# An adaptive-LayerNorm attention block with a gated low-rank adapter: one small matrix of gates for four rank groups, and context products spread between other work

## The chip, the cores and the metric

The kernel runs on one core of a Trainium2 chip. The metric is the device time of one execution in microseconds (us). The core's engines run side by side, each in its own program order, and wait for each other on semaphores: TensorE (PE in the profile, its weight loads PEld), VectorE (DVE), ScalarE (ACT), GpSimd (POOL), and SyncE (SP), which here issues the DMA transfers.

## What is computed

Input x has 1024 tokens of 512 columns, everything in float32. `c` gives six modulation vectors of 512 columns (shift and scale for two LayerNorms, and the gates ga and gb).

```
h = layernorm(x) * (1 + ca) + sa
q, k, v = h @ wq.T + bq, h @ wk.T + bk, h @ wv.T + bv     # 32 heads of 16 columns
# attention is over the 32 heads of one token, not over tokens
scores = einsum('bshd,bstd->bsht', q, k) / sqrt(16)
context = einsum('bsht,bstd->bshd', softmax(scores), v)
x = x + ga * context
h = layernorm(x) * (1 + cb) + sb
A_eff = einsum('bn,nri->bri', gate, lora_A)   # 8 groups b of 128 tokens, 16 adapters n, rank r = 32
B_eff = einsum('bn,nor->bor', gate, lora_B)
delta = einsum('bor,btr->bto', B_eff, einsum('bri,bti->btr', A_eff, h))
      + (h @ lora_A_shared.T) @ lora_B_shared.T
x = x + gb * (h @ kernel + bias + delta)
```

## The kernel before

**Tiling.** Tokens are handled in two halves of 512, and in eight groups of 128 in the second part. Each engine's order is written out by hand, in one function per engine. PSUM has eight banks of 128 x 512 float32; the list that `bank_plan` makes gives every use its bank in turn. TensorE's `take` waits until the use eight places earlier in that list has been emptied; the letter in the list says who empties it ("a" ACT, "v" DVE), and `emptied` counts in that order.

**Precision.** The projections and the last product split both operands into a high and a low part and take three passes of 512 columns. All other products are plain float32. Such a product appears in the trace as two passes, each with its own weight load; a transposition is one pass.

**First part.** LayerNorm, transposition, projections. For attention, k and v are copied by DMA into block-diagonal matrices `diag` (one per half), so that one product serves several tokens. `scores(k)`, softmax in four chunks per half (DVE maximum, POOL subtraction, ACT exponential, DVE sum, POOL multiplication, DVE `turn`), then `context(k)` (L1112): 64 products per half with 64 stationary columns (two slots of 32 heads) and 128 moving columns. One product writes partitions 0 to 63, the next 64 to 127. Half of what each computes pairs a slot with the other slot's values. ACT (`ctx_low_part`, L645) and DVE (`ctx_high_part`, L909) pick the right half with a mask, one pass each for every one of 16 banks, and POOL (`gate_ctx`, L488) multiplies by ga (`ga_col`).

**Order of TensorE around the change.** v of the second half (four banks), context(0), transposed lora_B (`b_t`), the two shared adapter matrices (`as_t`, `bs_t`), the transposed context of half 0 (`ctx_t`), `b_eff`, context(1), then for the second part `h2_t(0)`, `a_eff` chunks between halves of ctx_t(1), `h2_t(1)`, and the loop over eight token groups: `ax` (the adapter's first product), the output product with kern_hi and kern_lo, and two passes with `b_rows` (the adapter's second product).

**The adapter.** `gmix` holds gates: 128 rows (four adapters by 32 ranks) by 128 columns for each of four adapter groups and two halves of the token groups. `b_eff` and `a_eff` sum four such products per bank. The rows of `b_rows` are: own high part, own low part, shared high part, shared low part, each 32 partitions. SP fills them by DMA from `b_raw_hi`, `b_raw_lo` (L424, L426) and, for the shared rows, from `tail_hi` and `tail_lo` (L416, L418).

**Between the parts.** DVE adds the transposed context to x (`add_x`, L943), takes the statistics, normalises four token groups (L779), then `b_raw_lo`, then context(1)'s `ctx_high_part`. ACT does `h2_t` (modulation), `h2_high_part`, and `take_a`, which copies `a_eff` into `a_cat`. `split_h2` (L949) on DVE makes the low part of h.

## Time and profile before

| | |
|---|---|
| time of three runs | median 190.35 us (190.28 to 192.47) |
| the profiled execution | 191.63 us, of which the span from first to last instruction is 189.8 us |
| busy share of the span | PE 95%, PEld 81%, DVE 63%, ACT 55%, POOL 46% |
| instructions | 3335 in all; 1326 passes on PE |
| mean granted TensorE clock | 0.99 of full speed |

A row of a timeline gives the start and the length in us, the engine, the line of the kernel, the operation, the tile written and the tiles read, and how many instructions were merged into the row. In brackets stands how long the engine sat idle before and what ended that. Passes on PE are pipelined and overlap, so the time from one row's start to the next is the better measure of what a row cost.

### The profile page before, as it was taken

Reading aid. Unit: us, or ns where it says so; the run is one execution under the profiler, and the core shown is the slowest. Engines: PE = TensorE matmul, PEld = TensorE weight load, DVE = VectorE, ACT = ScalarE, POOL = GpSimd, SP = SyncE. Lnnn points to the kernel's source line nnn. Section 1 sums busy time; section 2 is a strip of 40 time slices with the busy share of each in tenths; the row PEclk is TensorE's granted clock in tenths of the full one; section 3 lists DMA queues with packets and bytes.
Section 4 is the critical chain, followed back from the end, with each engine's and each line's share of the span. In section 5 each row is a group of like instructions: output and inputs, shape, how many; then the busy total and the mean of one; then the engine's idle time right before and its main releaser. Section 6 shows DMA issues by size and latency. Waiting matters only on the chain.

```text
span 189.8 us, 3335 instructions
## 1 busy us (share of the span) xinstructions
PE 180.8 (95%) x1326; PEld 154.6 (81%) x1326; DVE 120.4 (63%) x193; ACT 104.5 (55%) x177; POOL 87.4 (46%) x59
## 2 busy tenths in 40 slices
PE   6997999799999999999999999999999899999993
PEld 6997778688778898888799879964989688888892
DVE  4674994792193277972026977579948587955543
ACT  8623914995124688354366486795674445444410
POOL 1000797099600297984007994945199042420000
PEclk9999699999999999999999999999999999999999
DMA  4999998968197059599859937969690001111112
GB/s 125 372 299 271 301 388 262 409 157 106 45 129 102 3 96 122 78 164 134 89 96 130 297 146 232 185 132 264 176 122 4 0 2 55 55 60 55 61 68 94
DMA packets 24848, 27.95 MB, mean 147 GB/s; under 512 B 12000, under 2 KB 16480, under 8 KB 24192
## 3 DMA queue, kind: packets, MB, share of 16 engines
q1 hardware_dynamic: 24832, 27.74, 63.1%
q8 instruction: 10, 0.16, 0.4%
q14 instruction: 6, 0.05, 0.1%
HBM read 17.24 MB, written 2.10 MB: 102 GB/s over the span
## 4 chain that ended last, share of the span: by engine, by line
PE 76%; DVE 10%; DMA 6%; POOL 3%; SPq 2%; issue 2%; ACT 2%; DVEq 0%
PE ps L1024 15%; PE ps L1026 15%; PE ps L1025 15%; PE ps L1108 8%; PE ps L1016 7%; DMA wm_attn<-in_L_wmod_dram 6%; PE ps L1205 4%; PE ps L1122 4%; PE ps L1161 3%; POOL ctx_c L491 3%; DVE xres L943 2%; DVE xn L779 1%; DVE wk_lo L792 1%; DVE wk_hi L789 1%; DVE stats L768 1%
## 5 line engine op out<-in xcount | busy, mean ns | idle before, releaser
L452 POOL MEMSET diag<- 128x2048 f32 x8 | 14.4, 1823 | 20.8 <-PE ps L1016 20.7
L477 POOL TENSOR_TENSOR steps<-steps,rmax 128x1024 f32<-128x1024 f32 x8 | 15.3, 1925 | 12.0 <-DVE rmax L889 12.0
L447 POOL TENSOR_TENSOR hT_lo<-h_full,hT_hi 128x512 fp32r<-128x512 f32 x8 | 12.1, 1528 | 18.5 <-ACT hT_hi L554 18.5
L698 ACT ACTIVATE h_full<-ps,modc 128x128 f32<-128x128 f32 x32 | 12.1, 456 | 13.3 <-PE ps L1016 13.3
L519 POOL TENSOR_TENSOR xres<-xres,bias_bc 128x512 f32<-128x512 f32 x8 | 12.3, 1563 | 13.0 <-DVE xn L779 13.0
L484 POOL TENSOR_TENSOR steps<-steps,rinv 128x1024 f32<-128x1024 f32 x8 | 15.3, 1918 | 3.8 <-DVE rinv L899 3.8
L889 DVE TENSOR_REDUCE rmax<-steps 128x32 f32<-128x1024 f32 x8 | 9.6, 1199 | 11.8 <-ACT steps L525 11.8
L562 ACT ACTIVATE k<-ps,b_col 128x512 f32<-128x512 f32 x8 | 9.3, 1184 | 12.6 <-PE ps L1026 10.2
L1108 PEld LDWEIGHTS ps<-diag,q 128*64 128x64 f32 x256 | 14.6, 192 | 1.2 <-issue 1.2
L1108 PE MATMUL ps<-diag,q 128*64 128x128 f32 x256 | 14.9, 277 | 0.6 <-issue 0.6
L1122 PEld LDWEIGHTS ps<-diag,steps 128*64 128x64 f32 x256 | 13.9, 137 | 1.1 <-issue 1.1
L1122 PE MATMUL ps<-diag,steps 128*64 128x128 f32 x256 | 14.4, 273 | 0.0
L628 ACT ACTIVATE steps<-steps 128x1024 f32<-128x1024 f32 x8 | 8.5, 1066 | 10.0 <-POOL steps L477 10.0
L1024 PE MATMUL ps<-kern_lo,h_hi 128*128 128x512 f32 (+1 forms) x36 | 14.0, 388 | 0.0
L1024 PE MATMUL ps<-hT_lo,wk_hi 128*128 128x512 f32 x32 | 13.6, 426 | 0.4 <-DVE wk_lo L792 0.4
L491 POOL TENSOR_TENSOR ctx_c<-ctx_c,ga_col 128x512 f32<-128x512 f32 x8 | 10.0, 1282 | 8.4 <-DVE ctx_c L913 8.4
L1026 PE MATMUL ps<-kern_hi,h_hi 128*128 128x512 f32 (+1 forms) x36 | 13.3, 370 | 0.0
L1025 PE MATMUL ps<-kern_hi,h_lo 128*128 128x512 f32 (+1 forms) x36 | 13.2, 366 | 0.0
L895 DVE TENSOR_REDUCE rsum<-steps 128x32 f32<-128x1024 f32 x8 | 9.7, 1216 | 5.3 <-ACT steps L628 5.3
L568 ACT ACTIVATE v<-ps,b_col 128x512 f32<-128x512 f32 x8 | 9.3, 1187 | 6.7 <-PE ps L1026 6.6
L1026 PE MATMUL ps<-hT_hi,wk_hi 128*128 128x512 f32 x32 | 12.7, 398 | 0.0
L1025 PE MATMUL ps<-hT_hi,wk_lo 128*128 128x512 f32 x32 | 12.7, 397 | 0.0
(140 smaller groups left out, 460.0 us busy)
## 6 DMA issues: line engine op xcount, KB each, us to landing
wm_next<-in_L_wmod_dram SPq DMA_DIRECT2D x3, 1024.0 KB, 8.9
x<-_attn_hidden_states_dram SPq DMA_DIRECT2D x8, 256.0 KB, 8.3
wm_attn<-in_L_wmod_dram SPq DMA_DIRECT2D x4, 512.0 KB, 7.7
diag<-k SPq DMA_DIRECT2D x16, 128.0 KB, 4.7
q<-q SPq DMA_DIRECT2D x16, 128.0 KB, 4.9
diag<-v SPq DMA_DIRECT2D x8, 256.0 KB, 7.3
xres<-_attn_hidden_states_dram SPq DMA_DIRECT2D x2, 1024.0 KB, 10.0
out_dram<-xres SPq DMA_DIRECT2D x7, 256.0 KB, 2.0
```

The source lines that it names most:

```text
L447: nc.gpsimd.tensor_tensor(hT_lo[k][:, c], h_full[:, c], hT_hi[k][:, c].bitcast(F32), ALU.subtract).then_inc(h_split, 1)
L452: nc.gpsimd.memset(diag_s[k][:, s, :], 0.0).then_inc(diag_zero, 1)
L477: nc.gpsimd.tensor_tensor(rows, rows, rmax[:, c % 2 * RCH:(c % 2 + 1) * RCH].unsqueeze(2).to_broadcast([P, RCH, H]), ALU.subtract).then_in ...
L484: nc.gpsimd.tensor_tensor(rows, rows, rinv[:, c % 2 * RCH:(c % 2 + 1) * RCH].unsqueeze(2).to_broadcast([P, RCH, H]), ALU.mult).then_inc(no ...
L491: nc.gpsimd.tensor_tensor(part, part, ga_col[:].unsqueeze(1).unsqueeze(1).to_broadcast([P, QUAD, n * GB, D]), ALU.mult).then_inc(ctx_gated, 1)
L519: nc.gpsimd.tensor_tensor(x_j, x_j, bias_bc[:], ALU.add).then_inc(biased, 1)
L1016: ins = nc.tensor.transpose(dst[0:m, n * k:(n + 1) * k], src, ident[0:k, 0:k])
L1024: nc.tensor.matmul(dst, a_hi, b_lo, start=start, stop=False)
L1025: nc.tensor.matmul(dst, a_lo, b_hi, start=False, stop=False)
L1026: return nc.tensor.matmul(dst, a_hi, b_hi, start=False, stop=stop)
L1108: ins = nc.tensor.matmul(dst[r, n * P:(n + 1) * P].rearrange("p (e c) -> p e c", c=IC), q2_g[:, g], diag_k[k][:, g], start=True, stop=True)
L1122: ins = nc.tensor.matmul(to[r, n], pT_g[k][:, g, r], diag_v[k][:, g, 2 * y:2 * y + 2], start=True, stop=True)
```

## The change

One `gmix` of 128 rows (16 adapters by 8 ranks) and 64 columns (8 ranks by 8 token groups) serves four groups of ranks. lora_A and lora_B are read in with their ranks regrouped so. `b_eff` becomes four products of 64 stationary and 512 moving columns, two side by side in one bank; `a_eff` becomes, per bank, four products of 128 stationary and 64 moving columns without summing. `context(c)` is now called for one softmax chunk at a time: 32 products with 32 stationary and 64 moving columns, whose outputs go to four different groups of 32 partitions, and which compute only what is needed. Eight banks hold what sixteen held. The masks and the passes on ACT and POOL go away; DVE's `gate_ctx` reads the bank and multiplies by ga. The eight calls of context stand between v, b_t, a_eff and h2_t. The shared B rows are made in partitions 64 to 127 (by a product with doubled `bs_nat`, in place of transpositions) and copied by POOL to all token groups, in place of two DMA transfers. ACT normalises token groups 2 and 3 in place of DVE; DVE's `b_raw_lo` moves ahead of the statistics; ACT's `kern_hi` moves ahead of `b_t`, and `take_a(0)`, `take_a(1)` ahead of `h2_t(0)`.

```diff
@@ bank_plan
-    uses += [("v", i, "a") for i in half(1, IC)]
-    uses += [("ctx", s, "v") for s in half(0, NSH)]
...
+    uses += [("v", IC, "a"), ("v", IC + 1, "a"), ("ctx", 0, "v"), ("v", IC + 2, "a"), ("ctx", 1, "v")]
...
@@ SP
-            sp.dma_start(la_nat, lora_a.rearrange("(c n) r i -> (n r) c i", n=NG)).then_inc(la_in, 16)
+            sp.dma_start(la_nat, lora_a.rearrange("n (e g) i -> (n e) g i", g=NRG)).then_inc(la_in, 16)
             v_to_diagonal(1)
-            sp.wait_ge(psum_written, written("ctx", NSH - 1))
-            sp.wait_ge(tail_hi_made, 1)
-            sp.dma_start(b_rows[2 * rank:3 * rank].bitcast(F32), tail_rows(tail_hi)).then_inc(b_tail_in, 16)
-            sp.wait_ge(*emptied("bs_t", 0))
-            sp.dma_start(b_rows[3 * rank:4 * rank].bitcast(F32), tail_rows(tail_lo)).then_inc(b_tail_in, 16)
             sp.wait_ge(v_diag_in[1], 16 * QUAD)
             sp.dma_start(xr[1], x_rows[:, NBH:NB, :]).then_inc(x_again[1], 16)
+            sp.wait_ge(psum_written, written("ctx", NCH - 1))
             for q in range(2):
-                tiles = slice(NG * q, NG * (q + 1))
+                own = slice(q * rank // 2, (q + 1) * rank // 2)
...
-                sp.dma_start(b_rows[0:rank, tiles, :].bitcast(F32), b_raw_hi[:, q, :].bitcast(F32)).then_inc(b_eff_in[q], 16)
+                sp.dma_start(b_rows[own].bitcast(F32), b_raw_hi[:, q, :].bitcast(F32)).then_inc(b_eff_in[q], 16)
...
@@ POOL
-            for s in range(0, NSH, 2):
-                gate_ctx(s, 2)
             pool.wait_ge(kern_hi_made, 1)
             nc.gpsimd.tensor_tensor(kern_lo, kern_nat, kern_hi.bitcast(F32), ALU.subtract).then_inc(kern_split, 1)
-            for s in range(NSH, 2 * NSH, 2):
-                gate_ctx(s, 2)
+            pool.wait_ge(kern_split, 1)
+            pool.wait_ge(psum_written, written("ctx", NCH - 1))
+            pool.wait_ge(tail_hi_made, 1)
+            pool.wait_ge(*emptied("bs_t", 0))
+            nc.gpsimd.tensor_copy(b_rows[2 * rank:], tail[2 * rank:, :].bitcast(F32).unsqueeze(1)
+                                  .to_broadcast([2 * rank, NB, hid])).then_inc(tails_made, 1)
...
@@ ACT
+            deviations(2, 0, 2)
+            deviations(3, 2, 4)
+            act.wait_ge(shift_ready, 2)
+            for n, j in enumerate((2, 3)):
+                nc.scalar.activation(xn2[:, j, :], xr[0][:, j, :], ACT.Identity, bias=shift[:, n:n + 1],
+                                     scale=rstd[:, j:j + 1]).then_inc(xn_by_act, 1)
...
+            take_a(0)
+            take_a(1)
             h2_t(0)
             h2_high_part(0)
-            take_a(0)
-            take_a(1)
-            h2_t(1)
             take_a(2)
             take_a(3)
+            h2_t(1)
@@ DVE
+            def gate_ctx(c):
+                dve.wait_ge(psum_written, written("ctx", c))
+                steps_c = slice(c % NCH * 2 * GB, (c % NCH + 1) * 2 * GB)
+                nc.vector.tensor_tensor(ctx_q[:, :, steps_c, :],
+                                        bank("ctx", c).rearrange("p (q g d) -> p q g d", q=QUAD, d=D),
+                                        ga_col[:].unsqueeze(1).unsqueeze(1).to_broadcast([P, QUAD, 2 * GB, D]),
+                                        ALU.mult).then_inc(dve_emptied, 1)
...
@@ PE
+            def context(c):
+                k, n0 = c // NCH, c % NCH * 2 * GB
+                if c % NCH == 0:
+                    pe.wait_ge(v_diag_in[k], 16 * QUAD)
+                pe.wait_ge(turned, c + 1)
+                to = take("ctx", c).rearrange("p (q g e c) -> p g q e c", q=QUAD, g=2 * GB, c=IC)
+                for n in range(2 * GB):
+                    for s in range(SLOT):
+                        r = slice(s * H, (s + 1) * H)
+                        ins = nc.tensor.matmul(to[r, n], pT_g[k][:, n0 + n, r], diag_v[k][:, n0 + n, s],
+                                               start=True, stop=True)
+                ins.then_inc(psum_written, 1)
...
-                for c in range(IC):
-                    ins = nc.tensor.matmul(dst, gmix[:, c, i * P:(i + 1) * P], b_t[:, c, :],
-                                           start=(c == 0), stop=(c == IC - 1))
+                for n in range(2):
+                    ins = nc.tensor.matmul(dst[n * P // 2:(n + 1) * P // 2, :], gmix[:], b_t[:, 2 * i + n, :],
+                                           start=True, stop=True)
...
-                    for c in range(IC):
-                        ins = nc.tensor.matmul(dst[:, 0:NB * rank], la_nat[:, c, i * P:(i + 1) * P], gmix[:, c, :],
-                                               start=(c == 0), stop=(c == IC - 1))
+                    for g in range(NRG):
+                        n = slice(g * GROUP * NB, (g + 1) * GROUP * NB)
+                        ins = nc.tensor.matmul(dst[:, n], la_nat[:, g, i * P:(i + 1) * P], gmix[:],
+                                               start=True, stop=True)
...
                 if j == 0:
-                    pe.wait_ge(b_tail_in, 16 * 2)
-                if j % NG == 0:
-                    pe.wait_ge(b_eff_in[j // NG], 16 * 2)
+                    pe.wait_ge(tails_made, 1)
+                    for q in range(2):
+                        pe.wait_ge(b_eff_in[q], 16 * 2)
```

How TensorE's order moves, from b_eff to the loop over the token groups. A row is a line, an operation, the tile written and the tiles read, the size written, and a count of equal instructions. First before, from b_eff (L1152) on; L1122 is context(1), L1161 is a_eff, and L1016 is a transposition (of `xn` for h2_t, of `ctx_c` for ctx_t(1)):

```order
L1152 MATMUL ps<-b_t,gmix 128x512 x8
L1122 MATMUL ps<-diag_57,steps_101 64x8x16 x64
L1016 MATMUL ps<-ident,xn_58 128x128 x4
L1161 MATMUL ps<-gmix,la_nat 128x256 x4
L1016 MATMUL ps<-ident,ctx_c 128x128 x8
L1161 MATMUL ps<-gmix,la_nat 128x256 x4
L1016 MATMUL ps<-ident,ctx_c 128x128 x8
L1016 MATMUL ps<-ident,xn_58 128x128 x4
L1161 MATMUL ps<-gmix,la_nat 128x256 x8
L1205 MATMUL ps<-h_full,a_cat_98 128x128 x2
```

And of the change, the same stretch from b_eff (now L1148); L1107 is one chunk of context, L1157 a_eff, L1002 a transposition:

```order
L1148 MATMUL ps<-b_t,gmix 64x512 x4
L1107 MATMUL ps<-diag_57,steps_100 32x4x16 x32
L1157 MATMUL ps<-gmix,la_nat 128x64 x4
L1107 MATMUL ps<-diag_57,steps_100 32x4x16 x32
L1157 MATMUL ps<-gmix,la_nat 128x64 x4
L1107 MATMUL ps<-diag_57,steps_100 32x4x16 x32
L1002 MATMUL ps<-ident,xn_58 128x128 x4
L1107 MATMUL ps<-diag_57,steps_100 32x4x16 x32
L1157 MATMUL ps<-gmix,la_nat 128x64 x8
L1002 MATMUL ps<-ident,ctx_c 128x128 x16
L1002 MATMUL ps<-ident,xn_58 128x128 x4
L1204 MATMUL ps<-h_full,a_cat_97 128x128 x2
```

h2_t(0) now stands ahead of the last chunk of context, and all of ctx_t(1) behind the last a_eff.

How DVE's order moves between the statistics of half 0 and add_x of half 1. Before, from the second normalisation (L779); L964 is b_raw_lo, L913 `ctx_high_part`, L943 add_x, L949 split_h2:

```order
L779 SCALAR_TENSOR_TENSOR xn_58<-xres_83,mv,rstd 128x512 x2
L964 TENSOR_TENSOR b_raw_lo<-ps,b_raw_hi 128x512 x2
L913 SCALAR_TENSOR_TENSOR ctx_c<-ps,half_mask,ctx_c 128x4x64 x8
L943 TENSOR_TENSOR xres_84<-ps,xres_84 128x4x128 x2
L949 TENSOR_TENSOR h_lo<-h_full,h_hi 128x512
L943 TENSOR_TENSOR xres_84<-ps,xres_84 128x4x128 x2
```

And of the change, from the one normalisation that is left (L764); L949 and L950 make rstd and shift for ACT, L895 is `gate_ctx`, L932 split_h2, L926 add_x:

```order
L764 SCALAR_TENSOR_TENSOR xn_58<-xres_82,mv,rstd 128x512 x2
L949 RECIPROCAL rstd<-std 128x2
L950 SCALAR_TENSOR_TENSOR shift<-mv,rstd 128x2
L895 TENSOR_TENSOR ctx_c<-ps,ga_col 128x4x128 x3
L932 TENSOR_TENSOR h_lo<-h_full,h_hi 128x512
L895 TENSOR_TENSOR ctx_c<-ps,ga_col 128x4x128
L926 TENSOR_TENSOR xres_83<-ps,xres_83 128x4x128 x4
```

split_h2(0) now stands ahead of the last gate_ctx, and the four steps of add_x behind both.

## Rows read from the trace of the kernel before

**Rows 1.** Page: busy time and share of TensorE; group of POOL memsets with mean ns.

```profile
PE 180.8 (95%) x1326; PEld 154.6 (81%) x1326; DVE 120.4 (63%) x193; ACT 104.5 (55%) x177; POOL 87.4 (46%) x59
...
L452 POOL MEMSET diag<- 128x2048 f32 x8 | 14.4, 1823 | 20.8 <-PE ps L1016 20.7
```

**Rows 2.** Chain that ended last, 113 to 152 us: start, length, what.

```profile
137.14 4.99 POOL ctx_c L491 x4
...
146.41 3.47 PE ps L1161 x16
```

**Rows 3.** Timeline of PE, 14 to 152 us: start, length, stationary*shape, moving size, passes.

```profile
16.07 1.95 PE L1059 MATMUL ps<-ones,wm_attn 128*128 128x1 f32 x16 [1.09 <-DVE wm_attn L819]
...
102.71 0.50 PE L1024 MATMUL ps<-hT_lo,wv_hi 128*128 128x512 f32 x1
...
113.80 7.21 PE L1122 MATMUL ps<-diag,steps 128*64 128x128 f32 x128
120.94 1.97 PE L1016 MATMUL ps<-ident,lb_nat 128*128 128x128 f32 x16
...
123.20 0.61 PE L1016 MATMUL ps<-ident,bs_nat 128*32 128x128 f32 x4
123.65 2.06 PE L1016 MATMUL ps<-ident,ctx_c 128*128 128x128 f32 x16
125.55 7.03 PE L1152 MATMUL ps<-b_t,gmix 128*128 128x512 f32 x16
...
150.61 1.16 PE L1205 MATMUL ps<-h_full,a_cat 128*128 128x128 f32 x8 [0.75 <-ACT a_cat L718]
151.53 0.48 PE L1024 MATMUL ps<-kern_lo,h_hi 128*128 128x512 f32 x1
```

**Rows 4.** Chain that ended last, 48 to 53 us: passes of one column.

```profile
49.09 1.68 PE ps L1088 x16
```

**Rows 5.** Timeline of DVE, 116 to 156 us.

```profile
116.51 1.25 DVE L907 STREAM_TRANSPOSE steps<-steps 128x1024 f32<-128x1024 f32 x1 [0.93 <-POOL steps L484]
...
125.08 3.92 DVE L943 TENSOR_TENSOR xres<-ps,xres 128x512 f32<-128x512 f32 x4
...
132.14 1.42 DVE L779 SCALAR_TENSOR_TENSOR xn<-xres,mv,rstd 128x512 f32<-128x512 f32 x2
...
135.00 1.28 DVE L964 TENSOR_TENSOR b_raw_lo<-ps,b_raw_hi 128x512 fp32r<-128x512 f32 x2
...
144.93 1.45 DVE L949 TENSOR_TENSOR h_lo<-h_full,h_hi 128x512 fp32r<-128x512 f32 x1
...
155.09 0.69 DVE L994 TENSOR_TENSOR gated<-ps,gb_bc 128x512 f32<-128x512 f32 x1
```

**Rows 6.** Timeline of ACT, 112 to 149 us.

```profile
112.74 2.40 ACT L568 ACTIVATE v<-ps,b_col 128x512 f32<-128x512 f32 x2
...
124.35 1.89 ACT L671 ACTIVATE kern_hi<-kern_nat 128x2048 fp32r<-128x2048 f32 x1
...
127.66 2.04 ACT L676 ACTIVATE a_cat<-ps 128x512 f32<-128x512 f32 x4
...
146.45 1.51 ACT L698 ACTIVATE h_full<-ps,modc 128x128 f32<-128x128 f32 x4 [0.68 <-PE ps L1016]
148.17 0.66 ACT L718 ACTIVATE a_cat<-ps 128x256 f32<-128x256 f32 x2 [0.22 <-PE ps L1161]
```

**Rows 7.** ACT groups by form: count, busy us, mean ns.

```profile
L580 ACT ACTIVATE x<-x,shift,rstd 128x512 f32<-128x512 f32 x3 | 2.2, 805 | 0.4 <-DVE shift L806 0.4
```

**Rows 8.** Timeline of POOL, 120 to 132 us.

```profile
126.32 4.56 POOL L513 TENSOR_TENSOR kern_lo<-kern_nat,kern_hi 128x2048 fp32r<-128x2048 f32 x1 [2.73 <-ACT kern_hi L671]
```

**Rows 9.** DMA issues, 117.14 to 117.6 us: KB, us to landing.

```profile
diag<-v SPq DMA_DIRECT2D x1, 256.0 KB, 8.7
```

**Rows 10.** DMA issues, 137.5 to 137.7 us.

```profile
b_rows<-b_raw_lo SPq DMA_DIRECT2D x1, 256.0 KB, 6.0
```

**Rows 11.** Stages: us, busy of five engines, clock, DMA share, GB/s.

```profile
18.90:22.30 3.40, 3.40 (x14) 2.88 (x13) 3.30 (x6) 3.40 (x6) 2.11 (x2) 0.52 1.06 258
```

More of the change, by code:

```diff
@@ L169, in adaln_block @@
         ones = sb("ones", P)
[L170 to L171 removed]
+        lora_mask = sb("lora_mask", lora_n)
+        group_mask = sb("group_mask", GROUP)
         root = sb("root", 1)
@@ L660, in _ @@
             project_v(IC + 3)
-            for s in range(NSH):
-                ctx_low_part(s)
+            act.wait_ge(kern_in, 16)
+            act.wait_ge(psum_written, written("v", 2 * IC - 1))
+            nc.scalar.activation(kern_hi, kern_nat, ACT.Copy).then_inc(kern_hi_made, 1)
             for i in range(IC):
@@ L666, in _ @@
             act.wait_ge(psum_written, written("bs_t", 0))
-            nc.scalar.activation(tail_hi[0:rank, :], bank("bs_t", 0)[0:rank, :], ACT.Copy).then_inc(tail_hi_made, 1)
-            act.wait_ge(kern_in, 16)
-            act.wait_ge(psum_written, written("v", 2 * IC - 1))
-            nc.scalar.activation(kern_hi, kern_nat, ACT.Copy).then_inc(kern_hi_made, 1)
+            nc.scalar.activation(tail[2 * rank:, :], bank("bs_t", 0)[2 * rank:, :], ACT.Copy).then_inc(tail_hi_made, 1)
             nc.scalar.activation(root[:], eps[:], ACT.Sqrt)
@@ L930, in _ @@
                     turn(c - 2)
-            for s in range(NSH):
-                ctx_high_part(s)
+            for c in range(NCH):
+                gate_ctx(c)
             dve.wait_ge(tail_hi_made, 1)
-            nc.vector.tensor_tensor(tail_lo[0:rank, :], bank("bs_t", 0)[0:rank, :], tail_hi[0:rank, :].bitcast(F32),
+            nc.vector.tensor_tensor(tail[3 * rank:, :], bank("bs_t", 0)[3 * rank:, :], tail[3 * rank:, :].bitcast(F32),
                                     ALU.subtract).then_inc(dve_emptied, 1)
@@ L956, in _ @@
             add_x(0, range(2, NCT))
+            for i in range(2):
+                dve.wait_ge(b_hi_made, i + 1)
+                nc.vector.tensor_tensor(b_raw_lo[:, i, :], bank("b_eff", i), b_raw_hi[:, i, :].bitcast(F32),
+                                        ALU.subtract).then_inc(dve_emptied, 1)
             dve.wait_ge(*emptied("ctx_t", NCT - 1))
@@ L960, in _ @@
             normalise(2, 0, 2, to_xn2, xr)
-            normalise(3, 2, 4, to_xn2, xr)
-            for i in range(2):
-                dve.wait_ge(b_hi_made, i + 1)
-                nc.vector.tensor_tensor(b_raw_lo[:, i, :], bank("b_eff", i), b_raw_hi[:, i, :].bitcast(F32),
-                                        ALU.subtract).then_inc(dve_emptied, 1)
-            for s in range(NSH, NSH + 4):
-                ctx_high_part(s)
-            for s in range(NSH + 4, 2 * NSH):
-                ctx_high_part(s)
-            add_x(1, range(2))
+            dve.wait_ge(std_ready, 4)
+            link(nc.vector.reciprocal(rstd[:, 2:4], std[:, 2:4]))
+            nc.vector.scalar_tensor_tensor(out=shift[:, 0:2], in0=mv_v[:, 2:4, 0], scalar=-1.0, in1=rstd[:, 2:4],
+                                           op0=ALU.mult, op1=ALU.mult).then_inc(shift_ready, 1)
+            dve.wait_ge(psum_written, written("ctx_t", NCT - 1))
+            for c in range(NCH, 2 * NCH - 1):
+                gate_ctx(c)
             split_h2(0)
-            add_x(1, range(2, NCT))
+            gate_ctx(2 * NCH - 1)
+            add_x(1, range(NCT))
             dve.wait_ge(*emptied("ctx_t", 2 * NCT - 1))
@@ L1184, in out_part @@
                                  start=False, stop=True).then_inc(psum_written, 1)
-            h2_t(0)
+            context(NCH)
             pe.wait_ge(la_in, 16)
             a_eff([0])
-            ctx_t(1, range(2))
+            context(NCH + 1)
             a_eff([1])
-            ctx_t(1, range(2, NCT))
+            context(NCH + 2)
+            h2_t(0)
+            context(NCH + 3)
+            a_eff([2, 3])
+            ctx_t(1, range(NCT))
             h2_t(1)
-            a_eff(range(2, IC))
             for j in range(NB):
```

140 lines of the change are left out of this document (53 added, 87 removed).

## The prediction

> **What bounds the kernel now.** I read the busy shares first: PE is busy for 180.8 us, 95% of the span [rows 1]. So the question is which PE work goes away, and whether PE finds its inputs in time once it has less to do. The chain of waits that ended last, read for the stretch of the change, runs through PE, but between the two contexts it leaves PE: DVE's add_x and normalisation, and POOL's gating (four passes, 4.99 us from 137.14) lie on it, then PE's a_eff [rows 2]. Both paths are about equally long there. The PE timeline gives what each piece costs [rows 3]. The four v projections of half 1 last from 102.71 to 113.80, 2.77 us each; context(0) 113.80 to 120.94, 7.14; b_eff 125.55 plus 7.03; the first output product (out(0)) starts at 151.53, after 0.75 us of waiting for ACT. From there the loop is PE's own to the end, so I look for the new start of out(0).
>
> **What PE loses and gains.**
> - b_eff: 16 passes of 512 columns in 7.03 us [rows 3], 0.43 each. Now 8 passes, of which two always write different halves of the partitions. Do such passes run side by side? Context shows it: 128 passes of 128 columns in 7.14 us are 0.056 each, while four passes with only 32 stationary columns, all to the same partitions, take 123.20 to 123.65, 0.11 each [rows 3]. A narrow pass is thus no faster alone, and two on different halves take the time of one. So 4 x 0.43 = 1.75 us, 5.3 less (3.5 if they took turns).
> - a_eff: 32 passes of 256 columns; the last 16 take 3.47 us [rows 2], 0.87 a bank. Now 64 columns, with full weights of 128 columns. What such a pass costs at least is seen where it moves one column: 16 passes in 1.68 us, 0.105 [rows 4]. With 0.11 a bank costs 0.9 instead of 1.75 us: 3.4 less in all.
> - bs_t: four transpositions become eight passes of 128 columns to the same partitions, at 0.11: 0.45 more.
> - Context: 64 products of 128 columns per half become 128 products of 64 columns, 256 passes. No row shows four groups of 32 partitions or a pass every 14 ns. Lower bound: all four groups side by side as the two are now; a pass of 64 columns then takes half as long, and four run at once: a quarter of 0.056, 14 ns each, 3.6 us a half. Upper bound: no pass starts faster than today's mean, 0.056, and a half takes 14.3 us. In between lies "no gain", 7.1 us. I take the lower bound, because the side-by-side running that it needs is what rows 3 show for two groups, plus 0.25 us for each of the eight calls, which now stand among other forms (estimate: 16 transpositions take 123.65 to 125.55, 0.119 each, against 0.112 for four narrow ones, so a start costs about 0.1). A call of context is then 0.9 + 0.25 = 1.15 us.
>
> **The path to out(0).** PE alone would gain 5.3 + 3.4 - 0.45 + 14.3 - 9.2 = 13.3 us. It cannot have all of this, since the others come in.
> - v4, v5, context 0, v6, context 1, v7: 102.71 + 11.1 + 2.3 = 116.1, 2.3 later than before. ACT empties v7 by 117.2, 2.1 later than 115.14 [rows 6]; kern_hi (1.89) follows.
> - Context 2 to 117.2; three b_t transpositions (sixteen took 1.9, [rows 3]) to 118.7. The fourth needs the bank of context 0, which DVE empties only behind its last `turn`, 116.51 + 1.25 = 117.76 [rows 5]; gate_ctx, a pass of 512 columns from PSUM, I price as the like pass at 155.09, 0.69 [rows 5]: 118.45. No wait. The two masks and POOL's gating go from the chain here. Context 3, as_t (0.36) and bs_t (0.9 + 0.1): 121.7, which in the trace was 123.65. tail_hi and tail_lo, 0.65 each, and DVE starts add_x at about 122.9, 2.2 earlier than 125.08 [rows 5].
> - From add_x to the end of the first two normalisations DVE took 125.08 to 133.56 [rows 5], 8.5 us; b_raw_lo (1.28) is now inside: 132.7. ACT hands it b_raw_hi in time: tail_hi to 122.3, the table load and a_cat 3.46 (from 126.24, the end of kern_hi, to 129.70, [rows 6]), two copies 1.1: 126.9, when add_x ends.
> - Reciprocal and shift 0.3: 133.0. Here a chain with ACT begins: two normalisations at 0.8 [rows 7] to 134.5, take_a(0) and (1) 1.3 to 135.8, h2_t(0) 1.51 to 137.3 [rows 6], h2_high 0.62 to 137.95; on DVE split_h2(0) 0.69 and the last gate_ctx 0.69: 139.3. Only then ctx_t(1) may start, since it waits for all four gate_ctx: 1.9 us, 141.2; h2_t(1) 0.5; ax(0) 0.92 (150.61 to 151.53, [rows 3]); **out(0) at 142.6, 8.9 earlier.**
> - Is PE ready? b_eff ends at 125.5. Context 4 waits for v's block-diagonal matrix: the last of its transfers took 8.7 us from 117.14 [rows 9], so 125.9, now 2.1 later with ACT's v7: 128.0. Context 4, a_eff 0, context 5, a_eff 1, context 6: 133.25; h2_t(0) at once, its input being there since about 132; context 7, a_eff 2 and 3: 136.7. PE then waits 2.6 us for ctx_t(1). The chain of DVE and ACT is the bound, not PE.
> - Behind out(0): DVE does add_x(1) (3.9), the statistics (1.55) and ax's low part (0.29) only after ctx_t(1) begins at 139.3, so that part is ready at 145.1 or later, and the twelve passes of out(0) end at 145.4. DVE also owes the rest of the first groups. I charge 1.0 us for such waits over three groups.
>
> Sum: 8.9 - 1.0 = **7.9 us less.** The profiled execution took 191.63 us, 1.3 above the median of 190.35; taken from the median this is 182.5.
>
> **Costed at nothing, and the cover.** POOL's copy of the shared rows, 4096 elements per partition: 3.65 us by the memset of 2048 elements in 1.82 [rows 1], 9.1 by kern_lo's two-input pass of 2048 in 4.56 [rows 8]. kern_lo comes 5 us earlier, so the copy ends between 127 and 133; it is needed at 145. Behind it queue POOL's bias additions. If one meets split_h2, that takes 1.45 instead of 0.69, as at 144.93 [rows 5]: 0.8 us, in the range. The four b_rows transfers now write 16 partitions instead of 32 and both must land before out(0) ends. One took 6.0 us [rows 10]; issued by 132 even twice that lands at 144. SP's two transfers of shared rows vanish ahead of them. The third lsh transfer lies at 29 us, far before its use.
>
> **A rule that speaks against it.** The row has 128 context passes at a mean of 56 ns, each with its own weight load, so it bounds the step between passes from above only [rows 3]. The Trainium skill (TensorE: Matmul & The Clock Gate, Back-to-back issue gap) gives a floor of about 25 ns from start to start however few columns move. By that a half would take 256 x 25 ns = 6.4 us instead of 3.6, and the sum would be about 185; its chance is part of the first rival's. No row here shows a mean under 56 ns.
>
> **The rivals.**
> - *Four groups bring nothing over two (18 in 100).* Context costs 7.1 us a half, as now, because passes to narrow groups are started no closer together in total: 2.05 us a call. For it: no row shows four. Against: rows 3 show two groups at the full pace. The same chain with 2.05: v7 at 117.9, add_x at 125.1, ctx_t(1) at 142.9, out(0) at 146.2, 5.3 earlier, less 1.0: **186.0**.
> - *Passes are bound by their number (10 in 100).* Each of 512 context passes takes 56 ns as today, 3.8 us a call. For it: that mean is the fastest in the trace. Against: two full passes side by side explain it without any bound on starts. PE is then never idle: v7 at 121.2, context 7 and a_eff end at 155, out(0) at 158.2, 6.7 later: **197**. Drawing a line between this and the rival above, the change loses from about 2.7 us a call on, 38 ns a pass.
> - *The clock falls in the new pause (15 in 100).* At 16.07, after PE had waited 1.09 us for DVE and then ran 16 passes of one column [rows 3], the clock went down: 18.90 to 22.30 was granted 0.52, so nearly all at the lower level, 1.2 GHz [rows 11]. The new PE waits are 2.5 and 2.6 us. One such stretch before out(0) costs half of 3.4: 1.7 us, **184.2**. Against it: only that once in 190 us.
>
> **How the numbers follow.** The forecast holds 52 in 100, with its own range of 181 to 184. Rivals hold 18, 10 and 15; the other 5 is a chain that is shorter than I think, below 181. From 180 to 187 all cases but the bound on passes and some tail are in, over 80 in 100. About 2% is what a measurement of this kernel can tell from no change, so faster means under 186.5: forecast, clock, the shorter chain and half of the first rival, 81, of which I keep 0.78 since several waits that I follow must all fit; 0.11 for no change and 0.11 slower.
>
> **What the new profile would show.** Right: one call of context lasts 0.9 to 1.2 us; b_eff 1.75 us, a_eff 0.9 a bank; out(0) starts near 142.6; PE's idle time before ctx_t(1) about 2.6 us, ended by DVE's gate_ctx; the loop of eight groups as long as before, within 1 us. Wrong: context calls over 2 us, or a pause ended by a transfer, by POOL's copy or by b_rows; a clock under 1 after 130 us.

## The result and the profile after

The changed kernel takes **187.84 us** (median of 187.23 to 189.59), the kernel before 190.49 in the same runs: a ratio of 0.9886, with an interval of 0.9845 to 0.9928. It is faster, by about 1%, where 182.5 (180.0 to 187.0) was forecast: just outside the range.

The profiled execution took 187.56 us. Its page, busy time and instructions of each engine, and further down the DMA queues (packets, MB, share of 16 engines), answers to [rows 1]:

```profile
PE 172.9 (93%) x1578; PEld 147.5 (80%) x1578; DVE 117.9 (64%) x184; ACT 100.5 (54%) x163; POOL 81.1 (44%) x52
...
q8 instruction: 12, 0.20, 0.5%
```

PE is 7.9 us less busy, with 252 passes and as many weight loads more, short ones. The timeline of PE shows the pieces, up to the next context, as [rows 3] did before:

```profile
101.23 0.50 PE L1010 MATMUL ps<-hT_lo,wv_hi 128*128 128x512 f32 x1
...
106.92 1.19 PE L1107 MATMUL ps<-diag,steps 128*32 128x64 f32 x64
...
120.19 1.09 PE L1139 MATMUL ps<-ident,bs_nat 128*64 128x128 f32 x8
121.21 2.07 PE L1002 MATMUL ps<-ident,ctx_c 128*128 128x128 f32 x16
123.22 1.94 PE L1148 MATMUL ps<-b_t,gmix 128*64 128x512 f32 x8
```

A context call lasts 1.19 us, 1.11 from its start to the next row's (forecast 1.15), b_eff 1.94 (1.75), and v starts at 101.23 instead of 102.71. The early part is thus 1.5 us earlier than in the profiled execution of before, which had a clock fall there [rows 11]; every forecast time is to be read 1.5 us earlier here. Not all of it is the clock: e2_pause_before (below), which up to there is the kernel before and had no such fall, starts v at 101.74, so about 1.0 goes with the fall and 0.5 is not placed. The chain that ended last (start, length, what) shows what came then:

```profile
118.73 9.18 DMA diag<-v
...
127.95 1.94 PE ps L1107 x64
129.88 1.90 PE ps L1157 x8
131.78 1.86 PE ps L1107 x64
133.65 1.90 PE ps L1157 x8
135.55 1.87 PE ps L1107 x64
137.42 0.93 PE ps L1002 x4
...
138.37 1.51 ACT h_full L684 x4
...
140.57 0.69 DVE h_lo L932
141.27 0.61 DVE ctx_c L895
...
141.92 0.73 PE ps L1002 x4
```

PE waits 2.80 us for v's block-diagonal matrix (the pause, from here on), and behind it each context call and each bank of a_eff (L1157) takes 1.9 us instead of about 1. Three rows of PE's timeline, with the waits and the start of out(0):

```profile
127.95 1.94 PE L1107 MATMUL ps<-diag,steps 128*32 128x64 f32 x64 [2.80 <-DMA diag<-v]
...
141.92 2.07 PE L1002 MATMUL ps<-ident,ctx_c 128*128 128x128 f32 x16 [0.54 <-DVE ctx_c L895]
...
145.34 0.49 PE L1010 MATMUL ps<-kern_lo,h_hi 128*128 128x512 f32 x1
```

The stages (us; busy time of five engines; granted clock; DMA share; GB/s) give the reason:

```profile
128.00:131.40 3.40, 3.40 (x72) 3.23 (x72) 3.30 (x10) 0.59 (x2) 0.00 (x0) 0.50 0.51 125
131.40:134.80 3.40, 3.40 (x72) 3.11 (x71) 3.15 (x6) 1.37 (x2) 3.09 (x3) 0.50 1.08 280
134.80:138.20 3.40, 3.40 (x72) 2.98 (x71) 0.69 (x1) 1.34 (x5) 2.30 (x2) 0.52 1.07 116
138.20:141.40 3.20, 3.18 (x82) 2.88 (x80) 0.83 (x2) 2.78 (x7) 0.00 (x0) 1.00 1.04 108
```

By the trace's clock records TensorE ran at its lower level, 1.2 GHz, for 10.24 us from 127.83 on, three times as long as the one stretch before [rows 11], though PE was busy from 127.95 on. out(0) starts at 145.34 (forecast, with the 1.5: 141.1). From there to the end of the span it takes 40.1 us, before 38.3.

### The profile page after: what moved, and what is told of

Read it like the earlier page. It is cut to its first block, busy times and chain, and to the rows that moved or that the text cites. A ratio compares the mean times of both kernels' runs of the same rounds, so it can differ in the third digit from the quotient of the medians.

```text
span 185.5 us, 3809 instructions
## 1 busy us (share of the span) xinstructions
PE 172.9 (93%) x1578; PEld 147.5 (80%) x1578; DVE 117.9 (64%) x184; ACT 100.5 (54%) x163; POOL 81.1 (44%) x52
## 4 chain that ended last, share of the span: by engine, by line
PE 65%; SPq 12%; DMA 9%; DVE 7%; ACT 4%; issue 2%; DVEq 0%
PE ps L1010 13%; PE ps L1011 13%; PE ps L1012 13%; PE ps L1094 8%; SPq L356 5%; DMA diag<-v 5%; PE ps L1107 5%; DMA b_col<-in_L_attn_bv_dram 4%; PE ps L1002 4%; PE ps L1204 3%; DVE xres L926 2%; ACT k L559 2%; PE ps L1157 2%; SPq L335 2%; SPq L342 1%
## 5 line engine op out<-in xcount | busy, mean ns | idle before, releaser
L484 POOL TENSOR_TENSOR steps<-steps,rinv 128x1024 f32<-128x1024 f32 x8 | 16.6, 2076 | 3.8 <-DVE rinv L882 3.8
L559 ACT ACTIVATE k<-ps,b_col 128x512 f32<-128x512 f32 x8 | 9.3, 1189 | 12.9 <-PE ps L1012 10.2
L625 ACT ACTIVATE steps<-steps 128x1024 f32<-128x1024 f32 x8 | 9.8, 1222 | 9.7 <-POOL steps L477 9.7
L1107 PEld LDWEIGHTS ps<-diag,steps 128*32 128x32 f32 x512 | 10.2, 134 | 5.3 <-DMA diag<-v 3.7
L565 ACT ACTIVATE v<-ps,b_col 128x512 f32<-128x512 f32 x8 | 9.8, 1272 | 8.3 <-PE ps L1012 8.3
L1107 PE MATMUL ps<-diag,steps 128*32 128x64 f32 x512 | 11.7, 259 | 2.8 <-DMA diag<-v 2.8
L1010 PE MATMUL ps<-hT_lo,wv_hi 128*128 128x512 f32 x32 | 12.8, 400 | 0.0
L1010 PE MATMUL ps<-hT_lo,wq_hi 128*128 128x512 f32 x32 | 12.7, 395 | 0.0
## 6 DMA issues: line engine op xcount, KB each, us to landing
diag<-k SPq DMA_DIRECT2D x16, 128.0 KB, 4.3
q<-q SPq DMA_DIRECT2D x16, 128.0 KB, 4.9
```

What stands on the lines that cost most here:

```text
L484: nc.gpsimd.tensor_tensor(rows, rows, rinv[:, c % 2 * RCH:(c % 2 + 1) * RCH].unsqueeze(2).to_broadcast([P, RCH, H]), ALU.mult).then_inc(no ...
L559: nc.scalar.activation(dst[i // IC][:, c], src, ACT.Identity, bias=b_col[:, n * IC + c:n * IC + c + 1]).then_inc(act_emptied, 1)
L1010: nc.tensor.matmul(dst, a_hi, b_lo, start=start, stop=False)
L1107: ins = nc.tensor.matmul(to[r, n], pT_g[k][:, n0 + n, r], diag_v[k][:, n0 + n, s], start=True, stop=True)
```

## The experiments

The theories. **A**: the pause lowers the clock, and the clock is what the forecast lacks. **B**: the narrow passes lower the clock, pause or not. **C**: the clock costs nothing, the chain over ACT and DVE sets the end. Two came up after the first runs. **D**: PE runs out of instructions, because their load waits behind data in the DMA queues. **E**: that load has a pace of its own, whatever the queues hold.

**Fill the pause with passes of no use.**

```diff
+            dst = take("ctx", NCH)
+            for n in range(12):        # e1_half: 6
+                nc.tensor.matmul(dst[:, 0:P], ones[:], ones[:], start=True, stop=True)
             context(NCH)
```

> The changed kernel with twelve matmuls of ones by ones (128x128 by 128 columns, float32) on TensorE ahead of the call for context 4, where it waits 2.80 us for v's second half; by the float32 passes of 128 columns elsewhere about 0.22 us each, 2.7 us together. Their result is overwritten by the context. Theory A (the pause brings the clock down, and nothing else): the granted clock stays at 1.0 from 125 to 146, the calls for contexts 4 to 6 take 1.0 to 1.2 us instead of 1.94, ctx_t(1) and out(0) come some 4 us sooner, and the kernel takes 183 to 184 us. Theory B (the narrow passes, 32 to 64 columns, bring it down or keep it down, pause or no pause): the calls still take 1.94 us from context 4 or 5 on and the time stays at 187 to 188. Theory C (the clock costs nothing, the end is set by the chain on ScalarE and VectorE): the clock is restored, the calls take 1.1 us, and the time still stays at 187 to 188.

> As the run with twelve fillers, but with six (about 1.3 us), so that about 1.5 us of the pause is left, 1.3 us less than the changed kernel has. Theory A with a clock that falls only for a long pause: the clock stays at 1.0 and the time is that of twelve fillers, 183 to 184. Theory A with any pause of over 1 us enough: the stretch at 0.5 begins behind the pause as before, and the time is 187 to 188. Theory B: 187 to 188 and a stretch at 0.5 here as well as with twelve.

Measured: twelve 191.56 us (ratio 1.0056, 1.0019 to 1.0093), six 190.52 (0.9981, 0.9956 to 1.0007): both slower than without. PE's timeline with twelve:

```profile
128.50 1.18 PE L1107 MATMUL ps<-diag,steps 128*32 128x64 f32 x64
...
130.65 1.18 PE L1107 MATMUL ps<-diag,steps 128*32 128x64 f32 x64
...
132.79 0.42 PE L1107 MATMUL ps<-diag,steps 128*32 128x64 f32 x13
136.73 1.71 PE L1107 MATMUL ps<-diag,steps 128*32 128x64 f32 x51 [3.52 <-issue]
...
144.43 1.76 PE L1157 MATMUL ps<-gmix,la_nat 128*128 128x64 f32 x8 [2.50 <-issue]
```

Its stages up to the first stop and into it:

```profile
128.00:131.40 3.40, 3.40 (x126) 3.11 (x128) 3.30 (x10) 0.58 (x2) 0.00 (x0) 1.00 0.64 162
131.40:134.80 3.40, 1.81 (x50) 1.50 (x41) 3.37 (x6) 0.80 (x3) 2.52 (x2) 1.00 1.05 232
```

The clock is 1.00 from 128 to 134.8 and the calls take 1.18 us, as A says. But in the middle of context 6, after 13 of 64 passes, PE stops for 3.52 us, and later for 2.50. "issue" means that it waits for nothing that the profile shows; no wait of the program stands there. With six, it stops 25 passes into context 6, for 1.75 us, and later for 3.72. None of A, B and C expected this.

**A pause in the kernel before.**

```diff
+            pe.wait_ge(xn_ready, XN_DVE + 4)
             context(1)
```

> The kernel before with one wait more: TensorE waits for the normalised rows 0 to 3 (VectorE, ready at 135.0) ahead of the second half's contexts, where it started at 132.5 without a wait. The work behind it is the wide one, 128 passes of 128 columns and 16 of 256 that the changed kernel no longer has. A pause of 2.5 us alone gives 190.4 + 2.5 = 192.9. Theory A (a pause of 2.5 us brings the clock down whatever follows): a stretch at 0.5 begins behind it; if that lasts 3.4 us as the one at 18.8 us did, the time is about 194.6; if it lasts 10 us as in the changed kernel, about 198. Theory B (only narrow work brings it down): the clock stays at 1.0 and the time is 192 to 193.

Measured: 192.96 us (1.0135, 1.0086 to 1.0185), 2.5 more than before. Timeline and stages:

```profile
134.11 7.21 PE L1122 MATMUL ps<-diag,steps 128*64 128x128 f32 x128 [2.50 <-DVE xn L779]
```

```profile
134.00:137.40 3.40, 3.29 (x60) 3.29 (x62) 2.22 (x5) 1.35 (x3) 0.20 (x1) 1.00 0.63 113
```

A pause of 2.50 us costs its own length here, and in the profiled execution the clock stays up. So a pause of this length is not enough by itself to bring the clock down.

**Real work in the pause.** Three banks of a_eff (their adapters landed at 121.3) go ahead of context 4; `bank_plan` follows.

```diff
+            pe.wait_ge(la_in, 16)
+            a_eff([0, 1, 2])
+            for c in range(NCH, 2 * NCH):
+                context(c)
+            h2_t(0)
+            a_eff([3])
-            context(NCH)
...
-            a_eff([2, 3])
@@ ACT: take_a(0) to (2) behind b_raw_hi. DVE: gate_ctx 4 to 7, add_x(1) in part, split_h2(0), the rest of add_x(1)
```

> The changed kernel with real work in the pause: the mixes a_eff 0 to 2 (about 0.95 us each at the full clock, 2.85 together; the adapters land at 121.3, so they wait for nothing) stand ahead of contexts 4 to 7, which then follow one another; ScalarE takes those three behind b_eff, VectorE gates contexts 4 to 7 ahead of the split of h2_t(0), which stands between the adds of x for the second half. Theory A: no pause over 0.5 us from 123 to 133, granted clock 1.0 throughout, contexts 4 to 7 end at about 132.7 instead of 139.4, ctx_t(1) starts at about 135.5 instead of 141.9, out(0) at 139 to 140 instead of 145.5; the loop's first group may then wait for the rows of b_eff (landed 137.7 to 143.1): 182 to 183 us. Theory B: the clock falls all the same when the narrow passes follow one another for 7 us, and the time is 185 to 187. Theory C: the time stays at 187 to 188 with the clock at 1.0.

Measured: 188.65 us (0.9876, 0.9837 to 0.9915), no better than the changed kernel. PE's timeline:

```profile
125.79 2.86 PE L1157 MATMUL ps<-gmix,la_nat 128*128 128x64 f32 x24 [0.50 <-ACT a_cat L665]
128.58 2.61 PE L1107 MATMUL ps<-diag,steps 128*32 128x64 f32 x157
136.45 2.99 PE L1107 MATMUL ps<-diag,steps 128*32 128x64 f32 x99 [5.26 <-issue]
```

The pause is gone, the clock was 1.00 until the stop, and yet PE stands still for 5.26 us inside context 6 (157 passes are two calls and 29 passes). The 2.8 us that were filled came back as a longer stop.

**What the stop is.** In e1_fill, e1_half and e3_mix_in_pause PE stops at the same instruction by number, the 2498th recorded one of PE and PEld, whatever work stands there: e1_half has six filler products less ahead than e1_fill, twelve passes, and stops twelve passes further on in context 6. e1_fill and e1_half stop again at 2754, 256 further on. The trace's packets have a queue for instructions (q8 on the page), which moves 16 KB at a time: 12 of them, for 3216 PE instructions, one for about 256 and so 64 bytes each. Where PE stands in its program and when the loads come, in these kernels and those that follow:

| us | PE at instruction 2242 | load starts, lands | PE at 2498 stops, goes on | next load | PE at 2754 stops, goes on |
|---|---|---|---|---|---|
| after (1.2 GHz) | 129.3 | 133.0, 133.9 | 136.4, no stop | 140.6, 142.5 | 143.7, 144.0 |
| e1_half | 129.0 | 132.2, 133.1 | 133.2, 135.0 | 142.2, 144.0 | 141.7, 145.4 |
| e1_fill | 129.0 | 133.2, 134.9 | 133.2, 136.7 | 141.3, 143.1 | 141.9, 144.4 |
| e3_mix_in_pause | 129.0 | 133.4, 134.7 | 131.2, 136.5 | 141.4, 143.2 | 143.4, 144.8 |
| e4_quiet | 129.9 | 130.5, 131.4 | 132.1, 132.9 | 134.2, 135.2 | no stop |
| e6_x1_late | 128.8 | 129.4, 130.6 | 130.9, 132.1 | 139.4, 141.1 | 138.5, 142.9 |
| e7_after_x1_late | 128.7 | 129.0, 130.0 | 135.4, no stop | 143.6, 145.1 | 142.3, 146.4 |
| e8_rows_early | 129.8 | 131.5, 133.4 | 131.9, 135.0 | 136.3, 137.1 | no stop |
| e9_stats_later | 129.0 | 131.2, 133.0 | 131.2, 134.3 | 135.7, 137.0 | no stop |
| e10_after_rows_early | 132.8 | 132.9, 134.0 | 139.0, no stop | 139.4, 140.4 | no stop |
| e11_after_stats_later | 130.3 | 134.0, 134.9 | 136.4, 136.6 | 143.1, 144.4 | 143.5, 145.9 |

PE goes on 1.3 to 1.9 us after a landing. For the second stops of e3 and e6 the profile names DVE's add_x as what ended them. The program does not wait for it there: h2_t(1) waits for rows that had long been normalised and for a bank that gate_ctx had emptied before ctx_t(1) began. e7 has the same stop at the same instruction, and there the profile says "issue". In e3_mix_in_pause two context calls, 256 instructions, pass in 2 us, while the load took from 129.0 to 136.5 to be of use.

**Empty queues, and fewer instructions.** To e3_mix_in_pause:

```diff
@@ e4_quiet, SP
+            sp.wait_ge(psum_written, written("ctx", 2 * NCH - 1))
             sp.dma_start(xr[1], x_rows[:, NBH:NB, :]).then_inc(x_again[1], 16)
-            sp.wait_ge(psum_written, written("ctx", NCH - 1))
@@ e5_half_calls, context()
-                    for s in range(SLOT):
+                    for s in range(SLOT if c < NCH else SLOT // 2):
```

> The kernel with a_eff 0 to 2 in the pause, with the loads of x's second half and of b_eff's rows issued only when the last context is done, instead of at 127.8 to 131.0. Nothing is left out; the end comes later because those rows are late, so only the stretch up to the last context counts here. The runs so far stopped TensorE without any wait of the program at one place of its instruction stream, whatever stood ahead in time (the 2498th recorded instruction, in three kernels, and again 256 instructions on), and each time it went on 1.3 to 1.9 us after a load of 16 KB on the instruction queue had landed. Theory D (TensorE runs out of instructions because that load, asked for at about 129, stands behind the 1 MB of x that was issued at 127.8): with the queues empty the load starts by 131 instead of 133.4, lands by 132.3, and the stop that lasted 5.3 us (131.2 to 136.5) shrinks to 1.5 to 3 us. Theory E (the load has a pace of its own, 8 to 10 us from one to the next, whatever the data queues do): it starts at 133 to 133.5 again and the stop is 5 us.

> The kernel with a_eff 0 to 2 in the pause, with only two of the four row groups computed in contexts 4 to 7 (16 of 32 products a call; the other half of those contexts is left out of the computation): 256 of TensorE's instructions less, one load of 16 KB, and at the full clock 1 to 2 us less of TensorE's time. Theory D and E (the number of instructions sets the pace): the place where TensorE stops moves behind the contexts, they end by about 132.5, the stop of 5.3 us is gone or falls on h2_t(0), out(0) comes at 140 to 141 instead of 146.4, and the time is 182 to 184. Theory C (ScalarE's and VectorE's chain sets it): out(0) comes no more than 1 to 2 us sooner, 185.5 to 187.

Measured, e4_quiet, one execution of 189.6 us (its end waits for the late rows), timeline:

```profile
129.46 2.59 PE L1107 MATMUL ps<-diag,steps 128*32 128x64 f32 x157
132.92 1.64 PE L1107 MATMUL ps<-diag,steps 128*32 128x64 f32 x99 [0.86 <-issue]
```

With no data in the queues the load starts 0.5 us after PE enters the last 256 instructions that it holds, instead of 4.3, and the stop is 0.86 us instead of 5.26. That is D; E is out. e5_half_calls, which leaves out half of the products of contexts 4 to 7, took 182.83 us (0.9595, 0.9557 to 0.9633), and its contexts stood in one row without a stop:

```profile
128.47 3.77 PE L1107 MATMUL ps<-diag,steps 128*32 128x64 f32 x128
```

They end at 132.2, h2_t(0) follows at once, and the next wait is DVE's gate_ctx, 2.23 us. This is the course of the forecast, and its time, with half of that work missing. 128 passes in 3.77 us, two groups of partitions side by side, are 29 ns each, against 17 with four groups: the products that were left out saved little of PE's time, and 256 of its instructions.

**The load of x issued later.** One line to e3_mix_in_pause (e6) and to the changed kernel (e7):

```diff
+            sp.wait_ge(psum_written, written("ctx", NCH))
             sp.dma_start(xr[1], x_rows[:, NBH:NB, :]).then_inc(x_again[1], 16)
```

> The kernel with a_eff 0 to 2 in the pause, and SyncE issues the load of x's second half (and b_eff's rows behind it) only when context 4 is written, at about 129.7 instead of 127.8, which is after TensorE has passed into the 256 instructions at which the next load of instructions is asked for (129.0). Theory D: that load starts by 131 instead of 133.4, the stop of 5.3 us shrinks to 2 to 3 us, x lands 2 us later (136 to 137), which the adds of x wait for at about 137 anyway, and the time is 184.5 to 186.5, against 187.4 without the wait. Theory E: the stop stays at 5 us, and x and the rows are 2 us later: 187.5 to 189.

> The changed kernel in its own order, with that wait alone: the load of x's second half is issued when context 4 is written (129.9 at the low clock) instead of at 127.9. TensorE ran at 1.2 GHz there from 127.8 to 138.1 and met the second load of instructions hardly at all. Theory D with the clock as the bound in that stretch: the time stays at 187 to 188, because TensorE at half the clock does not reach the end of its instructions. Theory E: the same or 1 us more, from x landing later.

Measured: e6_x1_late 187.59 us (0.9854, 0.9819 to 0.9889), e7_after_x1_late a ratio of 0.9856 (0.9817 to 0.9894). The first stop shrinks in e6 to 1.21 us, but the next load is due at 132.1, when x and three of the four copies of b_eff's rows are queued, starts 7.3 us later, and PE stops for 4.4. e6 missed its time by 1 us for that. In e7's profile TensorE, at 1.2 GHz for 6.8 us and not for 10.2, was 1.7 us earlier at ctx_t(1) (140.26 instead of 141.92), and then stood still for its instructions, so the gain was lost there. That execution took 190.43 us; those of 187.34 and 188.24 us, on which the ratio rests, have no trace, so whether they had this stop is not known:

```profile
140.26 2.07 PE L1003 MATMUL ps<-ident,ctx_c 128*128 128x128 f32 x16 [0.53 <-DVE ctx_c L896]
...
146.48 1.08 PE L1003 MATMUL ps<-ident,xn 128*128 128x128 f32 x4 [4.15 <-issue]
```

**Data in small portions between the loads.** To e3_mix_in_pause, SP only:

```diff
+            sp.wait_ge(psum_written, written("ctx", NCH - 1))
+            for q in range(2): ...  # b_raw_hi -> b_rows, each behind b_hi_made
             sp.wait_ge(v_diag_in[1], 16 * QUAD)
+            sp.wait_ge(psum_written, written("ctx", NCH))
             sp.dma_start(xr[1], x_rows[:, NBH:NB, :]).then_inc(x_again[1], 16)
+            sp.wait_ge(psum_written, written("ctx", 2 * NCH - 2))
+            for q in range(2): ...  # b_raw_lo -> b_rows
```

> The kernel with a_eff 0 to 2 in the pause, with SyncE's loads in another order: the two copies of b_eff's high rows as soon as ScalarE has them (125.9 and 126.4, where the queues are nearly empty), then x's second half when context 4 is written, then the two copies of the low rows when context 6 is written. The queues so hold less when TensorE asks for instructions: about 1 us of rows at 129.0, and x alone (about 4 us left) at 132.5 to 133. Theory D: the first stop is 1.5 to 2.5 us, the second, 4.4 us with x late alone, shrinks to 1 to 2; out(0) comes at about 141 to 142, and the time is 183.5 to 185. Theory E: both stops keep together 5.5 us or more and the time is 187 to 188.

Measured: **183.67 us** (0.9639, 0.9596 to 0.9681). The first stop is 3.10 us, longer than expected (rows are in the queue, and the load, due at 129.8, starts at 131.5), the second is gone, out(0) starts at 142.6:

```profile
134.97 2.91 PE L1109 MATMUL ps<-diag,steps 128*32 128x64 f32 x99 [3.10 <-issue]
```

The engines do the same work in the same order as in e3, which took 188.65. So C falls: the chain over ACT and DVE is not what held e3.

**And the order of DVE and ACT in the loop's first groups.**

```diff
@@ DVE, loop; ACT likewise h2_high_part(j + 1) ahead of deviations
-            layer_norm_stats(4, 6, xr)
...
-                if j == 1:
-                    layer_norm_stats(6, 8, xr)
                 if j < NB - 1:
                     split_h2(j + 1)
+                if j < 2:
+                    layer_norm_stats(2 * j + 4, 2 * j + 6, xr)
```

> The run with the rows early, and in the first two groups of the loop VectorE takes its low part of ax and the split of the next h2_t ahead of the statistics of x (1.6 us each), and ScalarE the high part of the next h2_t ahead of the deviations. In the changed kernel TensorE waits 0.31 us for VectorE's part of ax and 0.98 us for the split of h2_t(2) in those groups, and out(0) to the end takes 40.0 us, 1.75 us more than in the kernel before. If the order of VectorE's work is the cause of that, the loop takes 38.5 to 39 us and the time is 1 to 1.5 us less than with the rows early alone; if it is VectorE's whole work in those groups (4 us and more each), the normalised rows 4 to 7 only come later and the time is the same or up to 1 us more.

Measured: **182.85 us** (0.9604, 0.9583 to 0.9625), less than both kernels; the profiled execution took 182.52. One of its four executions took 186.11 and was granted 0.972 of the clock over its span, the others 0.991 or more; it has no trace, so where its clock fell is not known. In the profiled execution the narrow passes ran without a fall of the clock, so B is out. Its stages, with the stop of 3.11 us in the second one and the clock at 1.00 in all:

```profile
128.00:131.40 3.40, 3.17 (x164) 2.94 (x163) 3.35 (x6) 1.75 (x5) 0.00 (x0) 1.00 1.07 145
131.40:134.80 3.40, 0.53 (x37) 0.52 (x40) 3.31 (x8) 0.76 (x2) 2.16 (x2) 1.00 0.91 284
134.80:138.20 3.40, 3.40 (x99) 3.31 (x88) 2.21 (x5) 2.74 (x7) 3.33 (x3) 1.00 0.46 99
```

From the start of ax(0) to the end of the span it takes 40.9 us, e8_rows_early 41.8, the changed kernel 40.9, the kernel before 39.2. So the order is worth about 0.8 us, by the medians and by these spans, though the intervals of e8 and e9 overlap; what the other 1.7 over the kernel before consist of was not tried.

**Each of the two edits alone in the changed kernel's order.**

> The changed kernel in its own order on every engine but SyncE, whose loads come in the order that took the second stop away: high rows of b_eff when they are there, x's second half when context 4 is written, low rows when context 6 is written. The pause of 2.8 us stays, and the stretch at 1.2 GHz with it. Theory F (two limits, of which each hides the other: TensorE at 1.2 GHz takes until 138 for the contexts and a_eff, and at the full clock it would wait for its instructions about as long): prompt instructions alone bring nothing, 187 to 188. Theory D alone (the supply of instructions is the limit in the changed kernel, and the clock costs nothing because TensorE would wait anyway): 184 to 185.

> The changed kernel with the order of VectorE and ScalarE in the loop's first two groups alone: VectorE's part of ax and the split of the next h2_t ahead of the statistics of x, ScalarE's high part ahead of the deviations. TensorE's waits of 0.31 and 0.98 us there are 1.3 of the 1.75 us that the loop takes longer than before. If the order causes them: 186.3 to 187.0. If it is the amount of VectorE's work in those groups: 187.5 to 188.5.

Measured: e10_after_rows_early 187.58 us (0.9857, 0.9793 to 0.9921), e11_after_stats_later 188.21 (0.9881, 0.9804 to 0.9959): no change. In e10's profile loads cause no stop, but the pause grew to 5.09 us, since v's last transfer took 11.49 us instead of 9.18; that the early rows delayed it fits, but was not tried by itself. It is no clean measure of the clock:

```profile
131.37 1.94 PE L1109 MATMUL ps<-diag,steps 128*32 128x64 f32 x64 [5.09 <-DMA diag<-v]
```

In e11 the loop is 0.9 us shorter (40.0), and PE stops before h2_t(1):

```profile
145.93 0.63 PE L1001 MATMUL ps<-ident,xn 128*128 128x128 f32 x4 [2.43 <-issue]
```

So a reorder that is worth about 0.8 us behind e8 brings nothing here: in the profile the stop took it.

**Together.** Medians in us:

| | loads behind x and the rows | loads mostly ahead of them |
|---|---|---|
| pause kept, 1.2 GHz behind it | 187.84 (changed kernel) | 187.58 (e10; pause longer) |
| a_eff in the pause | 188.65 (e3) | 183.67 (e8) |

Neither cure alone brought anything, both together 4.2 us. That the full clock alone brings nothing is shown by e3. That prompt loads alone bring nothing rests on e10, where the pause was longer, so this half is read from the changed kernel's trace rather than isolated. Read so, the changed kernel has two limits in the same ten microseconds, and each hides the other: at 1.2 GHz PE meets instruction 2498 at 136.4, when its load has just become of use, and at the full clock it waits there for the load.

## Why the prediction was wrong

- **Right: the prices of the passes.** Four groups of 32 output partitions run side by side: 1.11 to 1.19 us a call against 1.15, b_eff 1.94 against 1.75, bs_t 1.09 against 1.0, a_eff 0.95 a bank at the full clock (2.86 for three in e3_mix_in_pause) against 0.9. The rivals "four groups bring nothing" (2.05 us a call) and "bound by their number" (3.8) fall with the first row. 64 passes in 1.1 us are 17 ns each. The Trainium skill (TensorE: Matmul & The Clock Gate, Back-to-back issue gap) has a floor of about 25 ns from start to start; across four groups of partitions the measurement goes below it, and decides. One reading in the prediction is a slip: "0.87 a bank" for a_eff before is half of what its row gives (3.47 us for two banks, 1.74 each); the sum uses 1.75, which is right.
- **Right: POOL's copy** took 3.60 us (lower bound 3.65) and ended at 127.4, and the rows landed in time.

```profile
123.76 3.60 POOL L510 CAST b_rows<-tail 64x4096 fp32r<-64x4096 f32 x1
```

- **Right in kind: the waits.** PE waited 2.80 us ahead of context 4 (2.5 forecast) for v, and ctx_t(1) waits for DVE's gate_ctx, though for 0.54 us and not for 2.6.
- **Wrong: "Is PE ready?"** This step ran contexts 4 to 6 and two banks of a_eff from 128.0 to 133.25, 5.25 us at the full clock, and concluded that the chain of DVE and ACT is the bound. It took 9.47 us (127.95 to 137.42), 4.2 more. With v 1.4 later than forecast this put h2_t(0) 5.6 us late, its four half-speed passes added about 0.5, and the slack of 2.0 us that the forecast had there is used up: ctx_t(1) started at 141.92 instead of 137.8, out(0) 4.2 late.
- **Mis-sized: the rival "the clock falls in the new pause".** The event was right, its price was not: one stretch of 3.4 us was copied from the only one in the trace [rows 11], and 10.24 us came. By its own rule, half of the stretch, that is 5.1 us before slack, not 1.7.
- **Missing: the instructions.** Without the clock the step would have failed all the same: e1_fill and e3_mix_in_pause had the full clock there and were no faster. The forecast counted what a pass costs once it is there, and made 252 more of them in shorter time; it never asked whether PE gets its instructions. In the kernel before 256 instructions lasted 12 us in that stretch (135.2 to 147.5), so a load's delay was hidden; in e3_mix_in_pause they last 2. In half 0, where the queues were nearly empty from 110 to 116, the changed kernel's load due at 111.8 started 0.7 us later, the contexts stood between projections, and the same calls ran without a stop. That is why the first call looked so good.
- **Mis-sized: the loop.** 1.8 us instead of the 1.0 charged: 0.31 us for DVE's part of ax, 0.98 for a split of h2_t; the other 0.5 is not placed. e9 and e11 give back 0.8 to 0.9.

```profile
148.65 0.47 PE L1178 MATMUL ps<-b_rows,ax_parts 128*128 128x512 f32 x1 [0.31 <-DVE ax_parts L964]
...
156.45 0.50 PE L1010 MATMUL ps<-kern_lo,h_hi 128*128 128x512 f32 x1 [0.98 <-DVE h_lo L932]
```

- The sum with what was measured, out(0) 4.2 late and the loop 1.8 longer: 8.9 less 4.2 less 1.8 is 2.9 us gained; the medians differ by 2.65. The 1.5 us of the early part are in neither.

Open: why the clock falls. In the profiles it fell behind pauses of 2.69 to 5.09 us before narrow passes (the changed kernel, e7, e10, e11), but also behind waits of 1.22 us (e1_half) and 2.23 us (e5) before transpositions, and in or behind stops of 2.50 us and more (e1_fill, e3, e6, e8). It did not fall behind 2.50 us before wide passes (e2), nor behind the stop of 3.11 us in e9, though it fell in e8's of 3.10. No run separates the length of the pause from the work beside it, nor tells why the stretch lasts 6.8 us in one run and 10.2 in another.

## What to carry to other kernels

Splitting products into many short ones buys time on the engine and spends instructions: multiply them out per microsecond, look at the packets of the instruction queue, and keep large transfers from being issued just before the next load falls due. Where a fix brings nothing, look whether another limit stands in the same place; here only both cures together paid. A stop that the profile calls "issue", at one and the same instruction number in several kernels, is a sign of it.
